# Layer-0 channel sum of a two-layer graph network: six fp32 matmuls in three 32-column strips, in place of added halves and three 48-column matmuls

## The reference

```python
h = 2.0 ** 0.5 * relu(emb @ W1 / 10.0 ** 0.5)              # E x 16 hidden channels
w = (h @ W2 / 16.0 ** 0.5).reshape(E, 7, 16, 8)            # seven 16x8 weights for each edge
s_out = PW_S * (einsum('eu,euw->ew', xs, wa_s) + INV_SQRT3 * einsum('eui,ei,euw->ew', xv, y1, wb_s))
g_out = ...   # the same with wa_g, wb_g
v_out = ...   # three sums with wc, wd, we -> 8 vectors of 3
edge_ftr = concat([tanh(s_out), tanh(g_out)[:, :, None] * v_out]) * norm
return segment_sum(edge_ftr, edge_dst, num_segments=N)
```

## Time and profile before

| | |
|---|---|
| time before, median of 3 runs | 6929.51 us (6928.4 to 6939.59) |
| the profiled execution | 6937.29 us, its span 6935.5 us |
| setup, until PE starts on the first group | about 571 us |
| first layer's edge loop | about 571 to 4138 us |
| what follows (node update, second layer) | about 4138 to 6935 us |
| busy share of the span: PE, DVE, ACT, POOL | 48%, 52%, 36%, 70% |

### The profile page before, as it was taken

How to read it: one execution, slowest core, us unless ns; L and a number is a source line. 1 busy time by engine, 2 the same in 40 slices (tenths; PEclk the granted TensorE clock), 3 DMA queues, 4 the chain that set the end, 5 groups by cost and what they waited for, 6 DMA issues and landing times. The chain is left out here.

```text
span 6935.5 us, 56399 instructions
## 1 busy us (share of the span) xinstructions
PE 3336.5 (48%) x12859; PEld 1619.6 (23%) x12859; DVE 3611.6 (52%) x5473; ACT 2498.8 (36%) x3555; POOL 4829.8 (70%) x4416
## 2 busy tenths in 40 slices
PE   0005999999999999999999980000000000000000
PEld 0003444444444444444444430000000000000000
DVE  4225888788887888888888862012222222212221
ACT  0005666666666666666666650000000000000000
POOL 4576777777777777777777628777666676677657
PEclk9999999999999999999999995555555555555555
DMA  3411111111111111111111101111111111111111
GB/s 138 160 39 36 30 28 30 30 29 30 30 30 30 30 28 27 31 31 29 30 31 30 23 13 11 12 21 25 26 27 21 29 25 24 24 25 25 24 26 20
DMA packets 275726, 228.08 MB, mean 33 GB/s; under 512 B 194512, under 2 KB 251465, under 8 KB 273006
## 3 DMA queue, kind: packets, MB, share of 16 engines
q0 software_dynamic: 131424, 79.08, 8.3%
q1 hardware_dynamic: 144082, 147.06, 6.6%
HBM read 137.03 MB, written 88.30 MB: 32 GB/s over the span
## 5 line engine op out<-in xcount | busy, mean ns | idle before, releaser
L1152 POOL DMA_INDIRECT gxb<-tab_d,idxb x1600 | 1537.3, 961 | 707.6 <-issue 626.2
L535 POOL DMA_INDIRECT gx<-in_x,idx x1540 | 1679.0, 1090 | 411.1 <-issue 368.4
L862 DVE TENSOR_TENSOR prod<-G_ps,hid 128x1000 f32<-128x1000 f32 x1200 | 1420.8, 1193 | 618.6 <-PE G_ps L738 303.9
L752 PE MATMUL R_ps<-sums,red 128*48 128x500 f32 x2400 | 1297.2, 624 | 0.0
L1244 PE MATMUL R_ps<-dm,ones 125*125 125x125 f32 x2 | 0.8, 494 | 2598.0 <-DVE dm L1273 2598.0
L631 ACT ACTIVATE FT<-T_ps 128x500 fp32r<-128x500 f32 x1200 | 707.0, 589 | 524.5 <-PE T_ps L721 323.0
L721 PE MATMUL T_ps<-ident,HL 125*128 125x125 f32 x4800 | 753.5, 280 | 270.1 <-ACT HL L625 189.5
L542 POOL TENSOR_TENSOR sums<-prod 128x500 f32<-128x500 f32 x400 | 502.7, 1257 | 516.3 <-DVE prod L862 312.4
L1159 ACT ACTIVATE ex<-ex 125x80 f32<-125x80 f32 x40 | 10.8, 269 | 2214.8 <-issue 1117.7
L1205 DVE TENSOR_TENSOR_SCAN Zb<-dec,Zb,wx 125x40 f32<-125x40 f32 x1280 | 333.3, 294 | 722.3 <-issue 721.3
L721 PEld LDWEIGHTS T_ps<-ident,HL 125*128 125x128 f32 x4800 | 574.1, 143 | 484.8 <-ACT HL L625 189.8
(11 more groups left out here) (190 smaller groups left out, 4268.7 us busy)
## 6 DMA issues: line engine op xcount, KB each, us to landing
y_d<-Zb SPq DMA_DIRECT2D x40, 664.1 KB
gx<-in_x,idx POOLq DMA_INDIRECT x1600
gxb<-tab_d,idxb POOLq DMA_INDIRECT x1600
xd_d<-zeros SPq DMA_DIRECT2D x16, 1562.5 KB
xv<-xd_d SPq DMA_DIRECT2D x40, 625.0 KB
y_d<-zr SPq DMA_DIRECT2D x40, 625.0 KB
em<-in_edge_attr SPq DMA_DIRECT2D x40, 195.3 KB
kp<-keep_d SPq DMA_DIRECT2D x40, 156.2 KB
```

The costliest lines, as they stand in the source:

```text
L535: nc.gpsimd.indirect_dma_start(out=gx[h][:, c * DIM:(c + 1) * DIM], out_offset=None, in_=x, in_offset=bass.IndirectOffsetOnAxis(idx[h][:, ...
L752: last = Tn.matmul(R_ps[0:NOUT, 0:GW], red[:, i * NOUT:(i + 1) * NOUT], sums2[k][:, i * GW:(i + 1) * GW], start=(i == 0), stop=(i == 2))
L862: V.tensor_tensor(prod[i][:, :].rearrange("p (a e) -> p a e", a=2), gv, hid[k][:, :].rearrange("p (a e) -> p a e", a=2), ALU.mult).then_in ...
L1152: nc.gpsimd.indirect_dma_start(out=gx[h][:, c * T1:(c + 1) * T1], out_offset=None, in_=tab_d, in_offset=bass.IndirectOffsetOnAxis(idx[h][: ...
```

## The change

The additions of halves go. `prod` becomes two sets (k = 0, 1) of three tiles; `sums2` is gone. PE sums over both partitions and halves: for each half j and each product i, one fp32 matmul with 32 output columns into partitions 32i to 32i+31 of `R_ps`, the second half accumulating on the first, so six matmuls stand in one block where three stood apart. `red` shrinks to two blocks of 32 columns, 16 of each 32 output rows holding results. The block stands at the place of the former reduce(n-1,1), and waits for the third multiply of its group. `rt` has 96 partitions; the transposes of `back` take 96 columns, reordered through the identity so that the 48 useful ones come first, and the next transpose overwrites the other 48. The positions of outputs in `Y_ps` change accordingly in `post`. multiply(n,0) waits for the sum of group n-2, which frees its `prod` set; the waits for the additions are gone.

```diff
@@ gpsimd
-                    def add(n, k):
-                        pool.wait_ge(S("b_mul"), n * 3 + 1)
-                        if not isinstance(n, int) or n > 1:
-                            pool.wait_ge(S("b_R"), n - 1)
-                        nc.gpsimd.tensor_tensor(sums2[k][:, 0:GW], prod[0][:, 0:GW], prod[0][:, GW:2 * GW], ALU.add).then_inc(S("b_addp"), 1)
@@ scalar
-                        A.activation(rt[k][:, :], R_ps[0:NOUT, 0:GW], ACT.Copy).then_inc(S("b_rt"), 1)
+                        A.activation(rt[k][:, :], R_ps[0:96, 0:GW], ACT.Copy).then_inc(S("b_rt"), 1)
@@ tensor
-                    def reduce(n, k, i):
-                        if i == 0:
-                            pe.wait_ge(S("b_addp"), n + 1)
-                            if some(n):
-                                pe.wait_ge(S("b_rt"), n)
-                        else:
-                            pe.wait_ge(S("b_add"), n + 1)
-                        last = Tn.matmul(R_ps[0:NOUT, 0:GW], red[:, i * NOUT:(i + 1) * NOUT], sums2[k][:, i * GW:(i + 1) * GW], start=(i == 0), stop=(i == 2))
-                        if i == 2:
-                            last.then_inc(S("b_R"), 1)
+                    def reduce(n, k):
+                        pe.wait_ge(S("b_mul"), n * 3 + 3)
+                        if some(n):
+                            pe.wait_ge(S("b_rt"), n)
+                        for j in range(2):
+                            for i in range(3):
+                                r0 = 32 if i == 2 else 0
+                                last = Tn.matmul(R_ps[32 * i:32 * i + 32, 0:GW], red[:, r0:r0 + 32], prod[k][i][:, j * GW:(j + 1) * GW], start=(j == 0), stop=(j == 1))
+                        last.then_inc(S("b_R"), 1)
@@ back
-                            last = Tn.transpose(Y_ps[0:P, (k * GT + c) * NOUT:(k * GT + c + 1) * NOUT], rt[k][:, c * P:(c + 1) * P], ident[0:NOUT, 0:NOUT])
+                            last = Tn.transpose(Y_ps[0:P, (k * GT + c) * NOUT:(k * GT + c) * NOUT + 96], rt[k][:, c * P:(c + 1) * P],
+                                                ident[0:96, 0:96].rearrange("p (i a f) -> p a i f", a=2, f=2 * MO))
@@ the turn of tensor
                             product(n, k, 2)
-                            if before:
-                                reduce(n - 1, 1 - k, 0)
                             if more1:
                                 hidden(n + 1, 1 - k, 1)
                             if more2:
                                 transposes(n + 2, g2, pc2, 1)
                             if before:
-                                reduce(n - 1, 1 - k, 1)
+                                reduce(n - 1, 1 - k)
                             if more1:
                                 product(n + 1, 1 - k, 0)
                             if more2:
                                 transposes(n + 2, g2, pc2, 2)
-                            if before:
-                                reduce(n - 1, 1 - k, 2)
@@ vector
-                        if some(n):
-                            if i == 0:
-                                dve.wait_ge(S("b_addp"), n)
-                            else:
-                                dve.wait_ge(S("b_add"), n)
+                        if i == 0 and (not isinstance(n, int) or n > 1):
+                            dve.wait_ge(S("b_R"), n - 1)
-                    def add(n, k):
-                        dve.wait_ge(S("b_mul"), n * 3 + 3)
-                        if not isinstance(n, int) or n > 1:
-                            dve.wait_ge(S("b_R"), n - 1)
-                        q = prod_t[:, 2 * GW:].rearrange("p (i a e) -> p i a e", i=2, a=2)
-                        V.tensor_tensor(sums2[k][:, GW:3 * GW].rearrange("p (i e) -> p i e", i=2), q[:, :, 0], q[:, :, 1], ALU.add).then_inc(S("b_add"), 1)
```

More of the change, by code:

```diff
@@ L83, in gnn_resnorm_kernel @@
         wh = sb("wh", [128, 2 * 128], f32r)
-        red = sb("red", [128, 3 * NOUT])
+        red = sb("red", [128, 2 * 32])
         attn_b = sb("attn_b", [P, 2 * DIM])
@@ L227, in _ @@
                     nc.gpsimd.memset(w1x[:, :], 0.0).then_inc(S("a_wh0"), 1)
-                    for i, (b, o0, nw, r0) in enumerate(((0, 0, 2 * MO, 0), (1, 3 * MO, 2 * MO, 0), (2, 2 * MO, MO, 0), (2, 5 * MO, MO, 64))):
-                        blk = red[:, b * NOUT + o0:b * NOUT + o0 + nw]
+                    for i, (b, o0, nw, r0) in enumerate(((0, 0, 2 * MO, 0), (1, MO, MO, 0), (1, 0, MO, 64))):
+                        blk = red[:, b * 32 + o0:b * 32 + o0 + nw]
                         nc.gpsimd.memset(blk, 1.0).then_inc(S("a_red"), 1)
@@ L445, in gnn_resnorm_kernel @@
             hid = [sbt(f"hid{k}", [128, 2 * GW]) for k in range(2)]
[L446 to L449, removed]
+            prod = [[sbt(f"prod{k}_{i}", [128, 2 * GW]) for i in range(3)] for k in range(2)]
+            rt = [sbt(f"rt{k}", [96, GW]) for k in range(2)]
             W2G = 2 * GT
@@ L559, in turn @@
                         for g in range(G2):
-                            add(t * G2 + g, g % 2)
                             if g % GC == 5 and not (last and g > GC):
@@ L808, in _ @@
                     back(NG - 2, 0)
-                    for i in range(3):
-                        reduce(NG - 1, 1, i)
+                    reduce(NG - 1, 1)
                     back(NG - 1, 1)
@@ L855, in multiply @@
                         dve.wait_ge(S("b_G"), n * 3 + i + 1)
[L856 to L869 removed]
+                        if i == 0 and (not isinstance(n, int) or n > 1):
+                            dve.wait_ge(S("b_R"), n - 1)
+                        gv = G_ps[(k * 3 + i) % 2][:, :].rearrange("p (a e) -> p a e", a=2)[:, :, 0:GW]
+                        V.tensor_tensor(prod[k][i][:, :].rearrange("p (a e) -> p a e", a=2), gv, hid[k][:, :].rearrange("p (a e) -> p a e", a=2), ALU.mult).then_inc(S("b_mul"), 1)
                     yv = Y_ps[0:P, 0:W2G * NOUT].rearrange("p (c f) -> p c f", f=NOUT)
@@ L884, in post @@
                                 dve.wait_ge(S("b_o"), m)
-                            V.tensor_tensor(pav, yv[:, :, 16:24].rearrange("p c (w a) -> p c w a", a=1).broadcast_to([P, W2G, MO, 3]),
+                            V.tensor_tensor(pav, yv[:, :, 40:48].rearrange("p c (w a) -> p c w a", a=1).broadcast_to([P, W2G, MO, 3]),
                                             drp[h][:, c0 * 3:(c0 + W2G) * 3].rearrange("p (c w a) -> p c w a", w=1, a=3).broadcast_to([P, W2G, MO, 3]),
@@ L891, in post @@
                             dve.wait_ge(S("b_pa"), m + 1)
-                            V.tensor_tensor(pbv, pav, yv[:, :, 24:48].rearrange("p c (a w) -> p c w a", a=3), ALU.add).then_inc(S("b_yr"), 2)
+                            V.tensor_tensor(pbv, pav, yv[:, :, 16:40].rearrange("p c (a w) -> p c w a", a=3), ALU.add).then_inc(S("b_yr"), 2)
                     def carry_sums(ch, h, t):
@@ L926, in turn @@
                                 post(1, pm, ph, pq, pt)
-                            add(n, k)
                             if feat:
```

1 line of the change is left out of this document (removed).

## The result

The changed kernel takes 7109.4 us (median of four runs, 7105.1 to 7119.37), the kernel before 6933.9 beside it: ratio 1.0257, interval 1.0241 to 1.0273. It is **2.6% slower**. The forecast was 6820 us and faster: the direction was wrong, and the time lies inside the range of 6640 to 7430 only because the range reached to the serial rival. That rival is not what happened. The strips ran side by side, and the time went elsewhere.

What follows compares the result with a forecast made beforehand. TensorE's issue order, 88% of the loop, plus three handoffs a chunk was taken as the bound. Middle case: -3.0 us a chunk times 40, -120 us, gives 6809; 11 for a drain makes 6820 us, range 6640 to 7430.

Steps and rivals of the forecast that it cites:

- serial rival: Block of six matmuls on TensorE: strips don't overlap, block 5.16 us, time 7365 us (7320 to 7430); chance 0.33.
- POOL running ahead at a price of nothing: POOL's gathers in the loop: without its addition they run ahead, with 1.6 us of slack, at no visible cost.
- middle case: Block on TensorE: each matmul's second record holds back the next strip; block taken as 3.3 us, -120 us; chance 0.40.
- drain at a switch of mode: Edges of the block on TensorE: growth bounded by 0 and 0.2 us each; 11 us added to the forecast.
- Rival 2: Block on TensorE: all three strips run side by side, 1.81 to about 2.25 us; 6620 us (6530 to 6730); chance 0.23.
- Rival 1's relief: In the serial rival, longer groups shorten waits by 8.7 of 19.6 us a chunk, leaving +436 us; chance 0.33.
- even groups' wait: TensorE's wait for late `T_ps` copies behind ACT's high parts: mostly hidden behind the block, -1.4 of 2.3 us a chunk.
- Rival 3: New handoff at T(n+2,2), DVE's first multiply fitting in 2.5 us: up to 0.4 us a chunk, within the middle case's range.
- bursts' wait: TensorE's wait in two groups a chunk for relu behind ACT's whole-chunk copies: stays, -0.3 of 5.0 us a chunk.
- Group 5's wait: TensorE's 1.67 us wait for a multiply behind DVE's `along`: -1.3 us, plus -1.0 for the clock; below 0.5 left.
- added waits: Block's wait for the third multiply, `b_rt`, and multiply(n,0) for the sum of n-2: never late or no cost.
- `back` with 96 columns: `back` transposes on TensorE, 96 columns instead of 48: 0 to 0.1 us, taken as 0.

Runs made afterwards that it cites:

- no_gathers: The changed kernel without the row gathers of the first layer's loop (first rows reused, other output): 6665 us, beside 6932 before the change.
- pace4: The changed kernel with POOL waiting in every group for its first multiply, ahead of the four gathers: 6777 us, ratio 0.9773 to the kernel before.
- pace4_add: pace4 plus a POOL addition of 128x500 on data nobody needs, ahead of each group's gathers: 6623 us in one run, beside 6929 before the change.
- early_pace4: pace4 with the block of six matmuls moved directly behind product(n,2): 6780 us, ratio 0.9789 to the kernel before.
- b_dveadd: The kernel before, without strips, with POOL's addition given to DVE so that POOL runs ahead: 7018 us, beside 6932 for the kernel before.
- wide48_pace4: pace4 with the six matmuls 48 columns wide, all into one place instead of strips: 7957 us, beside 6932 before the change.
- after_again: The changed kernel unedited, run on a chip where the kernel before takes 6700 us: 6435 us, ratio 0.9614.
- early_block: The changed kernel with only the block of six moved directly behind product(n,2), on a 6700 chip: 6200 us beside 6696, ratio 0.9261 to the kernel before.

## Why the prediction was wrong

**The step that failed: POOL running ahead at a price of nothing.** The text said that taking POOL off the chain "frees nothing by itself", that its gathers had 1.6 us of slack, and that the price of running ahead lay "between nothing and nothing I can see". The slack holds: no wait of the loop is put down to a row that came late. But I asked only what POOL waits for and who waits for POOL. What its gathers do to others while they are issued has no row among the releasers of POOL; it stood in the trace of before as three waits on "remote", 10.7 us in the loop, and as DVE's 236.4 us in the second layer (last section), which I passed over. It costs 446 us of loop on the 6930 chip (3745 - 3299), against -266 for everything else. That the gathers take part is shown by taking them away (no_gathers), and that POOL's order changes the size by pace4 and pace4_add. POOL's order does not set it alone: early_pace4 has that of pace4 and 536 us late instead of 285, b_dveadd has rows of eight and 87 us instead of 580. On the 6700 chips the same gathers, in the same rows of eight, delay no completion.

**The middle case for the block fell.** I let the second record of a matmul hold back the next strip, for 3.3 us. It holds back nothing: three records start together, the second and third 7 and 13 ns after the first, and four such rounds with the edge, 4 x 0.418 + 0.14, give the 1.81 us measured. Against the 5.16 us of wide48_pace4 that is 2.85 times. The Trainium skill, "TensorE: Matmul & The Clock Gate", "Measured speedup vs the span model", has 2.38 for three column strips; here the measurement decides, for fp32. From the same page's section "The mechanism" I had drawn that the order of the program forbids it; starts in order, nanoseconds apart, are just as strict an order. The Trainium skill, "TensorEngine Tiling (Array Packing)", "Key Properties", states a drain at a switch of mode, without a figure. The trace shows none near the 0.2 us that I allowed for: transposes to block take 0.57 us, 0.05 more than in the earlier trace rows, and the block's own edge is 0.14 as before.

**Rival 2 had the mechanism and nearly the size.** It gave 6620; no_gathers has 6665, after_again a ratio of 0.9614, which is 265 us of 6700 against its 309. A chunk takes 3291 / 40 = 82.3 us, inside its 79 to 84 (though its parts as listed come to 79 to 81 only, and the two waits below are larger than it had them, so part of the hit is luck). I gave it 0.23 because one argument from the order of records outweighed what the trace could not show; with the row silent, the three lengths deserved nearer chances.

**Rival 1's relief fell too.** Its block is right, 5.16, but wide48_pace4 has 11.47 us per group, where its +436 us meant 10.0. The waits for `T_ps` and `H_ps` that a longer group was to shorten grew by 194 and 102 us over the loop, 0.7 us a group: as I read the rows, a copy of `T_ps` is late by what stands directly ahead of its user in the order, and a longer block elsewhere in the group doesn't help it.

**The waits.** The even groups' wait was to hide (-1.4 us of 2.3 a chunk). TensorE's waits for the copies of `T_ps` grew instead, from 45.8 / 40 = 1.1 to 320.6 / 40 = 8.0 us a chunk on a chip without late completions: a reduce left the place between transposes 0 and 1, and the block stands behind both. Rival 3 looked for this handoff one step later. The bursts' wait, which was to lose 0.3 us a chunk, grew likewise, from 83.4 us to 220.7. early_block confirms that the place of the block matters: moving it gives -231 us. So a second term, the new handoffs, was mis-sized; it did not decide the sign, since the changed kernel is faster on the 6700 chips in spite of it. Group 5's wait went from 64.6 / 39 = 1.66 to 38.8 / 36 = 1.08 us, not below 0.5. The granted clock of the loop is 0.92 after, 0.97 before and 0.96 in after_again, so its fall came with the late completions and not with the strips.

**Right were** the added waits (weight loads of the block behind DVE, 17.3 us in all, 0.17 each), `back` with 96 columns, no longer than before, DVE's -1.48 and POOL's -1.33 us per group, and the second layer, unchanged at 2797 us.

## What to carry to other kernels

Before an engine that issues many indirect gathers is taken off the others' path, look in the trace for waits released by "remote" in a program of one core: here they marked late completions, and a wait or an instruction between the gathers was worth more than the time that it cost. After removing steps from an engine's written order, count again what stands between each producer and its consumer, since a removed step was also distance. And a difference of 3% on one chip may turn its sign on another.

## What the runs showed of the hardware

- Six fp32 matmuls of 500 columns in three 32-column strips: 1.81 us; the same count, 48 columns wide, into one place: 5.16 us. At two switches a group no edge grew by more than 0.05 us.
- TensorE's completions reached DVE and ACT up to 10.8 us late while POOL issued gathers of rows, on one chip: 580 us in sum with rows of eight gathers and strips, 285 with the wait per group, 44 with an addition besides, 87 with rows of eight and no strips, 5 without gathers; none on three other chips. In the second layer DVE's own completions reached DVE up to 9.5 us late, 509 us in sum in the kernel before, with TensorE idle; none on the other chips. The cause inside the chip is not settled.
- Those three chips run the kernel before in 6695 to 6700 us instead of 6930. In the changed kernel 230 us lie behind the loop (2572 us instead of 2802), in code that is the same in both kernels, so the loop of before, which has no trace there, should take about as long as on the 6930 chip (an estimate from these times). Behind the loop POOL pauses up to 13.2 us between gathers on the 6930 chip, and never over 0.3 us on a 6700 chip. The kernel before, second layer, 4330 to 6400:

```profile
POOL gxb L1152 <- issue: 535.5, 1363, 13.2
...
DVE rst L1182 <- remote: 236.4, 25, 10.1
```

and after_again:

```profile
POOL gxb L1127 <- issue: 457.4, 1501, 0.3
```

So on the 6930 chip the same "remote" stands in code that the change does not touch.
